# A bias moved from TensorE to ScalarE, and the last turn and tail of a pipelined layer put in another order

## What is computed

```python
xn = layernorm(x)
z, xBC, dt = split(xn @ in_proj_w.T)
xBC = silu(causal_conv4(xBC) + conv_b)
theta = clip(theta_base + tanh(xn @ w1) @ w2)
log_z = complex(-(lam + eta * theta**2) * dt, theta * dt)
S[t] = exp(log_z[t]) * S[t-1] + B[t] * (x[t] * dt[t])
y = real(C[t] . S[t]) + x * D
g = y * silu(z); g = g * rsqrt(mean(g*g) + eps) * norm_w
out = x + g @ out_proj_w.T + ffn(xn)      # ffn: three +-1 layers with relu
```

## Time and profile before

| what | us |
|---|---|
| median of 3 runs (335.78 to 337.73) | 336.48 |
| the profiled execution, its own time | 337.05 |
| its span, first to last instruction | 334.9 |
| TensorE busy | 292.5 (87%) |
| VectorE busy | 257.8 (77%) |
| GpSimd busy | 190.9 (57%) |
| ScalarE busy | 182.1 (54%) |
| TensorE's share of the chain that ended last | 65% |

### The profile page before, as it was taken

One profiled execution on the slowest core, in us unless ns is written; L12 is line 12 of the kernel. 1 busy time (PEld: TensorE's weight loads), 2 busy tenths in 40 slices (PEclk: granted clock), 3 DMA queues, 4 the chain that ended last, 5 costly groups with the idle time before them and its releaser, 6 DMA issues.

```text
span 334.9 us, 9439 instructions
## 1 busy us (share of the span) xinstructions
PE 292.5 (87%) x3927; PEld 210.1 (63%) x3927; DVE 257.8 (77%) x632; ACT 182.1 (54%) x336; POOL 190.9 (57%) x165
## 2 busy tenths in 40 slices
PE   1396679799999999999999999999899999968780
PEld 1253246587588758776678657875777577735680
DVE  4585788889788887988698878987798868887221
ACT  0587646287438844785567654774288445750110
POOL 1004253529990999279944997099918991684001
PEclk9879799999999999999999999999999999998795
DMA  7302300141012200230123001311022002301001
GB/s 204 82 0 50 78 0 2 33 97 33 31 35 68 61 18 25 77 78 2 33 57 91 16 31 41 76 45 33 3 64 66 3 31 50 81 0 34 2 2 37
DMA packets 19306, 14.85 MB, mean 44 GB/s; under 512 B 5077, under 2 KB 15034, under 8 KB 19258
## 3 DMA queue, kind: packets, MB, share of 16 engines
q1 hardware_dynamic: 17192, 13.83, 16.0%
q10 hardware_dynamic: 2066, 0.36, 0.6%
HBM read 3.70 MB, written 2.10 MB: 17 GB/s over the span
## 4 chain that ended last, share of the span: by engine, by line
PE 65%; DVE 10%; POOL 7%; ACT 6%; issue 3%; DMA 3%; SPq 2%; ACTq 1%; POOLq 0%; DVEq 0%
PE bank L1483 10%; PE bank L1534 7%; PE bank L1535 6%; PE bank L1585 4%; PE bank L1646 4%; PE bank L1545 4%; PE bank L1592 4%; PE bank L1555 4%; PE bank L1621 3%; PE bank L1636 3%; PE bank L1565 3%; ACT z L1107 2%; PE bank L1601 2%; PE bank L1523 2%; SPq L439 2%
## 5 line engine op out<-in xcount | busy, mean ns | idle before, releaser
L1332 POOL TENSOR_TENSOR btmp<-cims,X 128x512 f32<-128x512 f32 x15 | 19.1, 1272 | 68.0 <-DMA cims<-bc 53.0
L1534 PE MATMUL bank<-h0h,W 128*128 128x512 f16 x128 | 50.3, 393 | 6.9 <-DVE h1l L808 5.5
L1535 PE MATMUL bank<-h0l,W 128*128 128x512 f16 x128 | 50.0, 391 | 0.0
L1483 PE MATMUL bank<-XW,xh 128*128 128x256 f16 x256 | 48.3, 277 | 0.0
L1483 PE MATMUL bank<-XW,xl 128*128 128x256 f16 x128 | 35.3, 276 | 0.0
L1157 ACT ACTIVATE h1h<-bank 128x512 f16<-128x512 f32 x32 | 18.9, 593 | 22.7 <-PE bank L1535 22.7
L808 DVE SCALAR_TENSOR_TENSOR h1l<-bank,h1h 128x512 f16<-128x512 f32 x32 | 21.9, 687 | 11.0 <-ACT h1h L1157 10.9
L1483 PEld LDWEIGHTS bank<-XW,xh 128*128 128x128 f16 x256 | 25.3, 99 | 6.8 <-issue 0.2
L1534 PEld LDWEIGHTS bank<-h0h,W 128*128 128x128 f16 x128 | 13.9, 108 | 23.1 <-DVE h1l L808 7.0
L1113 ACT ACTIVATE tin<-bank,base 128x256 f32<-128x256 f32 x16 | 6.7, 472 | 36.5 <-PE bank L1508 36.5
L1307 POOL TENSOR_TENSOR xd<-x,dt 128x1024 f32<-128x1024 f32 x8 | 15.2, 1903 | 19.6 <-ACT x L1082 19.0
(11 more groups left out here) (196 smaller groups left out, 846.7 us busy)
## 6 DMA issues: line engine op xcount, KB each, us to landing
xtok<-in_x SPq DMA_DIRECT2D x8, 256.0 KB, 3.1
cres<-bc SPq DMA_DIRECT2D x32, 64.0 KB, 2.1
cims<-bc SPq DMA_DIRECT2D x32, 64.0 KB, 2.1
bres<-bc SPq DMA_DIRECT2D x32, 64.0 KB, 2.1
bims<-bc SPq DMA_DIRECT2D x32, 64.0 KB, 2.1
out<-osb SPq DMA_DIRECT2D x8, 256.0 KB, 2.3
const<-constants SPq DMA_DIRECT2D x1, 512.0 KB, 5.7
KT<-in_in_proj_w ACTq DMA_DIRECT2D x1, 320.0 KB, 4.5
```

The costliest lines, as they stand in the source:

```text
L1332: P.tensor_tensor(btmp[1][:], b[:], f2, ALU.mult).then_inc(sig.sem, 1)
L1483: last = M.matmul(dst, tok(x, c, k), w[:, k, :], start=False, stop=(k == TAPS - 1 and q == 2))
L1534: M.matmul(bank[4 + f % 2][:], w, h0h[:, k, :], start=(k == 0), stop=False)
L1535: last = M.matmul(bank[4 + f % 2][:], w, h0l[:, k, :], start=False, stop=(k == MT - 1))
```

## The change

**Bias.** The bias matmuls (L1481) go, for all sequences but 0. ScalarE writes conv_b times the scale into banks 7 and 6 ahead of the products (`x_bias`, two `ACTIVATE` of 128x512 a turn, one ahead of `decay_down`, one ahead of `dt_exp`), and `x_part` waits for that and accumulates. Sequence 0 keeps a matmul of one fp32 row. conv_b is loaded into all 128 partitions (128 KB for 1 KB), and the two operations that split it go from the setup.

**Steady turn.** `cims` is repeated before `cres`, with semaphores of their own; `trig` makes `psn` ahead of `Abs`; `states` moves behind `phases`.

**Last front turn.** `mlp0` and `mlp1` get banks of their own, `out_products` bank 7. `mlp1` tile 3 and `mlp_out` go to the tail. VectorE does `gated` after `exponents`, and `decayed(n, 2)` ahead of `b_and_k_im` and `final`. GpSimd no longer waits for `Uim` and `Bim`.

**Tail.** `last_tail`: `skipped` ahead of `new_states` and `within`; gate, squares and output by halves of the width, the sums ahead of the second half's output. The flag is formed ahead of the gate; SyncE loads it ahead of the last store, stores in two parts, and waits for landing after its branch.

```diff
-            (cb_row[:], a["conv_b"][0:INNER].rearrange("(o c) -> o c", o=1)),
+            (conv_bias[:], row_all(a["conv_b"], INNER)),
...
+        states_in_tail, out_in_last = bank[0], bank[7]
         mlp_in_bank = {True: bank[7], False: bank[4]}
+        mlp_in_last = bank[2]
+        MLP_BANKS = [bank[4], bank[5], bank[4], bank[5]]
+        MLP0_LAST = [bank[4], bank[5], bank[2], bank[6]]
+        MLP1_LAST = [bank[4], bank[2], bank[6], bank[2]]
+
+        def is_last(n):
+            return isinstance(n, int) and n == SEQS - 1
...
-                repeat_rows(STATE, cres, c_in)
-                repeat_rows(STATE + 1, cims, c_in)
+                repeat_rows(STATE + 1, cims, ci_in)
+                repeat_rows(STATE, cres, cr_in)
...
-                for p in range(2):
-                    store(SEQS - 2 + p, SEQS - 2 + p, p)
-                for p in range(2):
-                    sp.wait_ge(o_out[p], 16 * (SEQS // 2) + 1)
+                store(SEQS - 2, SEQS - 2, 0)
                 flag = general_needed(sp)
+                for part in range(2):
+                    sp.wait_ge(s_fin.sem, s_fin.at(SEQS - 1, 2 * part + 2))
+                    sp.dma_start(out_dram[SEQS - 1][:, 2 * part:2 * part + 2, :], osb[1][:, 2 * part:2 * part + 2, :]).then_inc(o_out[1], 16)
...
                 with nc.Else():
+                    for p in range(2):
+                        sp.wait_ge(o_out[p], 16 * (SEQS // 2 + p) + 1)
...
+            def flag_raised():
+                v.wait_ge(set_pe, 2)
+                V.tensor_reduce(top[:], bank[3][0:1, 0:128], AX_X, ALU.max).then_inc(flag_top, 1)
...
+                V.tensor_copy(again[:], above[:]).then_inc(flag_ready, 1)
...
                 def gates(slot):
                     gated(n - 1, pq)
-                    if has_front:
-                        h0_low(n, 0)
-                        h0_low(n, 1)
+                    h0_low(n, 0)
+                    h0_low(n, 1)
 
                 def low_tiles():
                     h0_low(n, 2)
                     h0_low(n, 3)
 
-                def new_states(slot):
-                    if slot == 1:
-                        states(n - 1)
-
-                if has_next:
-                    early_layernorm(n + 1)
-                if has_front:
+                if not has_front:
+                    masks()
+                    add_mlp(n - 1, (n - 1) % XBUFS)
+                    states(n - 1)
+                    flag_raised()
+                    gated_by_halves(n - 1, pq)
+                    mean_squares(n - 1)
+                    final(n - 1, pq, stored)
+                    return
+                if not has_next:
                     masks()
                     thetas(n)
-                    phases(n, new_states)
-                    exponents(n, True, gates, low_tiles)
-                else:
-                    masks()
+                    phases(n)
                     states(n - 1)
+                    exponents(n, True)
                     gates(3)
-                if has_next:
-                    xn_low(n + 1)
-                if has_front:
                     decayed(n, 0)
-                if has_back:
+                    low_tiles()
+                    decayed(n, 1)
+                    h1_low(n, 0)
                     mean_squares(n - 1)
-                if has_front:
-                    h1_low(n, 0)
-                    decayed(n, 1)
-                if has_front and not has_next:
                     b_times_rotated_im(n)
+                    decayed(n, 2)
                     h1_low(n, 1)
-                    final(n - 1, pq, stored)
+                    b_and_k_im(n)
                     h1_low(n, 2)
-                    decayed(n, 2)
+                    final(n - 1, pq, stored, out_in_last)
                     h1_low(n, 3)
-                    b_and_k_im(n)
-                    add_mlp(n, n % XBUFS)
                     largest()
                     return
-                if has_front:
-                    h1_low(n, 1)
-                if has_next:
-                    dt_input(n + 1)
-                if has_next:
-                    dt_steps(n + 1)
-                if has_back:
-                    final(n - 1, pq, stored)
-                if has_front:
-                    h1_low(n, 2)
-                    h1_low(n, 3)
-                    decayed(n, 2)
-                if has_next:
-                    bc_taps(n + 1)
-                if has_front:
-                    add_mlp(n, n % XBUFS)
+                early_layernorm(n + 1)
+                masks()
+                thetas(n)
+                phases(n)
+                states(n - 1)
+                exponents(n, True, gates, low_tiles)
+                xn_low(n + 1)
+                decayed(n, 0)
+                mean_squares(n - 1)
+                h1_low(n, 0)
+                decayed(n, 1)
+                h1_low(n, 1)
+                dt_input(n + 1)
+                dt_steps(n + 1)
+                final(n - 1, pq, stored)
...
-            setup(V.memset(CB[:], 0.0))
...
-            pair(CB[0:1, :], CB[BLK:BLK + 1, :], cb_row[:], BIAS_SCALE)
...
+            def x_bias(n, half):
+                if not (isinstance(n, int) and n < 2):
+                    act.wait_ge(s_gate.sem, s_gate.done(n - 2))
+                step(a_bias, A.activation(bank[6 + half][:].rearrange("p (c e) -> p c e", e=INNER),
+                                          view(conv_bias, 0, 128, 0, [[0, 2], [1, INNER]]), ACT.Copy, scale=PS))
...
+                step(a_trig, A.activation(psn, phl[:], ACT.Sin, scale=TURN))
                 step(a_abs, A.activation(pabs[:], phl[:], ACT.Abs))
-                step(a_trig, A.activation(psn, phl[:], ACT.Sin, scale=TURN))
...
+                    act.wait_ge(s_gate.sem, s_gate.at(n, 2 * half + 2 if is_last(n) else half + 3))
...
                     trig(n)
+                if has_front and not has_next:
+                    mlp_high(a_h0, t_h0, h0h, n, (0, 1), MLP0_LAST)
+                    decay_up(n)
+                    mlp_high(a_h0, t_h0, h0h, n, (2, 3), MLP0_LAST)
+                    squares(n - 1)
+                    decay_down(n)
+                    mlp_high(a_h1, t_h1, h1h, n, (0,), MLP1_LAST)
+                    range_checked(n)
+                    mlp_high(a_h1, t_h1, h1h, n, (1, 2, 3), MLP1_LAST)
+                    return
...
+                if has_next:
+                    x_bias(n + 1, 1)
+                if has_front:
...
+                    x_bias(n + 1, 0)
                     dt_exp(n + 1)
...
-                    if later_factor and k == 0:
-                        g.wait_ge(*later_factor)
+                    if k == 0:
+                        for awaited in later:
+                            g.wait_ge(*awaited)
...
+                elif last:
+                    c_rotated(n)
+                    b_times_rotated(n, True)
                     rms_of(n - 1)
...
+                    b_and_k(n, s_kq, 0, True)
+                elif has_front:
+                    c_rotated(n)
+                    b_times_rotated(n, between=lambda: rms_of(n - 1))
+                    b_and_k(n, s_kq, 0)
+                    b_and_k(n, s_kq, 1)
...
+                    if not first:
+                        pe.wait_ge(a_bias.sem, a_bias.at(n - 1, 2 - half))
...
-                if k == 0:
-                    M.matmul(dst, biasrow[:], CB[:], start=True, stop=False)
+                if first and k == 0:
+                    M.matmul(dst, scale_row[:], conv_bias[0:1, :], start=True, stop=True)
                 for q, (x, w) in enumerate(pairs(XW)):
-                    last = M.matmul(dst, tok(x, c, k), w[:, k, :], start=False, stop=(k == TAPS - 1 and q == 2))
+                    last = M.matmul(dst, tok(x, c, k), w[:, k, :], start=False, stop=True,
+                                    skip_group_check=True)
...
-                    if f >= 2:
+                    if f >= 2 and banks is MLP_BANKS:
                         pe.wait_ge(s_h0l.sem, s_h0l.at(n, f - 1))
...
+            def last_out_and_sums(n):
+                for half in range(2):
+                    pe.wait_ge(s_gate.sem, s_gate.at(n, 2 * half + 2))
+                    if half == 1:
+                        pe.wait_ge(a_gsq.sem, a_gsq.at(n, 1))
+                        sums_of_half(n, 0)
+                        pe.wait_ge(a_gsq.sem, a_gsq.done(n))
+                        sums_of_half(n, 1).then_inc(t_ms.sem, 1)
+                    for c in range(NCH):
+                        last = M.matmul(out_in[:, D * c:D * c + D], gT[:, half, CH * c:CH * c + CH], OW[:, half, :],
+                                        start=(half == 0 and c == 0), stop=True, skip_group_check=True)
+                last.then_inc(t_o.sem, 1)
...
+            def last_tail(b, p):
+                pe.wait_ge(s_msq.sem, s_msq.done(b - 1))
+                pe.wait_ge(s_h1l.sem, s_h1l.at(b, 1))
+                pe.wait_ge(s_kq.sem, s_kq.done(b))
```

(39 more changed lines are left out.)

183 lines of the change are left out of this document (105 added, 78 removed).

## The result

The changed kernel takes 327.47 us (median of 4 runs, 323.62 to 329.88), the kernel before 336.74 (4 runs, 335.78 to 337.73). The ratio is 0.969, 95% interval 0.960 to 0.978: **3.1% faster**, where 4.3% was forecast. The median lies 5.5 us above the forecast and 0.5 above the range. The profiled execution took 327.39, its span is 325.6 us against 334.9.

A forecast was written before the change was run, and what follows sets the result against it. TensorE's own length bounds the steady turn, GpSimd's loop nearly as long. 337.05 + 0.6 - 6.3 - 7.2 - 0.75 - 1.3 = 322.1; forecast 322.0 us, range 318.5 to 327.0.

The forecast's parts named there:

- Setup: Before the steady turns: two operations go, row loads and four fp32 bias matmuls cost more; 0.6 us more in sum.
- The start: Setup: two `CB` operations gone save 0.8 us, larger row loads cost 0.4.
- The clock rival: Tail after the last front turn: granted clock falls again, two stretches of 1.5 us each, 325.1; chance 0.14.
- The slower rival: From the gate's wait in the last front turn, clock stays at 1.2 GHz to the end: 341.1; chance 0.03.
- The bias in steady turns: TensorE's steady turns without bias matmuls: 1.15 us a turn worked out, 1.05 taken, 6.3 less over six.
- GpSimd's loop: Steady turn: reordering ends GpSimd 1.2 us earlier, 0.8 to spare; worth nothing alone, keeps the 6.3 us.
- A late landing as in the fifth turn: Steady turn: a late C transfer, as at 12.95 us after turn start, costs about what it costs now.
- The last front turn: Last front turn: TensorE starts the tail's G products at 300.65 instead of 307.91, 7.2 us less.
- The conflict with GpSimd: Last front turn: VectorE's `b_times_rotated_im` slowed beside GpSimd's product, 0.5 us added.
- the rival of three blocked operations: Last front turn: VectorE's three `b_times_rotated_im` operations each wait 1.27 us for GpSimd, 325.4; chance 0.08.
- most of this is order: Last front turn: most of the 7.2 us comes from `mlp1` tile 3 and `mlp_out` (1.96) no longer standing ahead.
- Tail and end: G products to `final`: 0.75 us less; after `final`: 1.3 less, VectorE ending the kernel 4.5 after it.

The follow-up runs named there:

- seq0_128rows: The changed kernel with sequence 0's fp32 bias matmuls over all 128 rows, scale/128 in each, instead of one row: 318.48 us.
- seq0_16bit: The changed kernel with sequence 0's bias again as the 16-bit product of a 33-row pair: 323.66 us.
- steady_old: The changed kernel with the old steady-turn order (cres before cims, Abs before psn, states inside the phases): median 331.64 us.
- bias_on_pe: The changed kernel with all sequences' bias again a 16-bit TensorE matmul per quarter, without ScalarE's two writes a turn: 330.0 us.
- all nine: Nine traces with the 128-row kernel's last front turn and tail unchanged; from turn start to the end of `final` they take 45.46 to 46.77 us.

## Why the prediction was right in sign and 5.5 us off

**Setup: the step that failed.** The prediction booked "0.25 each, 1.0 in all" for four one-row fp32 matmuls and 0.6 for the whole stretch. They cost 0.83 each, 3.3 in all, since all four fell into half clock. The price had been taken from a full-clock row (0.70 in the earlier trace rows), and at full clock it is right: 0.44 against 0.21 in `seq0_128rows` and `seq0_16bit`. But the trace showed the clock low up to 20.9, and the first bias matmul starts at 18.68. The prediction also asked only what the matmuls cost, not what they do to the clock of the work around them. That term stood at nothing and was 4.5 us: `seq0_128rows`, with all rows filled, takes 7.79 us for the quarters instead of 15.28. The start was the third miss, 0.9 us later where 0.4 earlier was booked. Together with 0.2 behind the quarters that is 8.9 for 0.6. The other stretches gave back 2.65 us net over what was booked, which leaves the 5.65 us of the span.

**The clock rival had the wrong place.** It was priced for the last front turn, where the clock did not fall at all (1.00 from 276.95 to 315), and it said 325.1 with a chance of 0.14. The mechanism, half clock on TensorE's own path, decided 4.5 to 7.8 us at the other end of the kernel. The slower rival (the clock stays low to the end) named a lasting low clock and had it only behind the last turn's start; lasting it was, for 20 us instead of the 3.4 of the earlier trace rows.

**The bias in steady turns: right.** 1.17 a turn against 1.15 worked out; the 0.1 kept back for `lora1` was not needed, and ScalarE's writes took 0.59 (booked 0.7) and stayed hidden.

**GpSimd's loop: right, and undersold.** "Worth nothing alone; it keeps the 6.3 us": `steady_old` loses 3.0 of 7.0 us, 0.5 a turn, and `bias_on_pe` shows that the order alone moves no turn of ordinary length. "A late landing as in the fifth turn costs about what it costs now" holds too: both kernels have room up to 11.7 us after the turn's start. The fifth turn gave back 1.2 us beyond the sum because no landing of the profiled execution was that late, which is luck and not the new order's doing; in `seq0_16bit`, with the same steady turn, one cost 0.96.

**The last front turn: right in size, wrong in its reason.** 7.0 against 7.2; `decayed(n, 2)` ended at 301.41, 0.2 later than placed. The conflict with GpSimd fell on `tmpa` (1.58 instead of 0.68, 0.9 where 0.5 was booked), which met a wide GpSimd operation at work, `U<-btmp`, up to 298.22. `tmpb` (0.68) ran beside `rms`, a product of 128x4. The third (0.69) was at work when GpSimd began `btmp<-K,bres`, and there GpSimd took longer, 1.39 instead of the 1.06 of the steady turns. So the rival of three blocked operations (325.4) did not come: one of three was held up. It rested on the Trainium skill, page SBUF — State Buffer, section Who interferes with whom, by which the loser is blocked while the other's instruction lasts. The one case here agrees: `tmpa` ended at 298.77, 0.55 behind `U<-btmp`.

But "most of this is order: `mlp1` tile 3 and `mlp_out` no longer stand ahead" is not a gain for the kernel: the first returns in the tail, net 0.1. VectorE's order is worth 1.4 of it by the two traces, and 0.3 to 1.6 against all nine. What the rest divides into (the gate's place, the banks, `mlp_out`) was not tried.

**Tail and end.** -0.4 against -0.75, with the halves worth 1.7 by the two traces and 0.5 to 1.7 against the nine. The end brought twice what was booked (2.6 against 1.3): VectorE's load of the flag does not wait for `final`, and took 0.54 us instead of 0.85, so SyncE's landing (2.6 us from the last store) ends the kernel together with VectorE, not VectorE 4.5 us behind.
